# A decoder layer on one core: the second residual and its statistics, done for three batches of rows during the masked attention

## What is computed

```python
x = _layernorm(x + _L0_attn_ref(x, Wq, bq, Wk, bk, Wv, bv, Wf, bf))      # x1
x = _layernorm(x + _L0_xattn_ref(x, ctx, ctx, mask))                     # x2, the change is here
x = _layernorm(x + _L0_ffn_ref(x, w_gate, w_up, w_down))

def _layernorm(x, eps=1e-05):
    m, v = jnp.mean(x, -1, keepdims=True), jnp.var(x, -1, keepdims=True)
    return (x - m) / jnp.sqrt(v + eps)

def _L0_xattn_ref(q, k, v, mask):      # q = x1, k = v = context; per head of 32 columns
    scores = jnp.where(mask == 0, -1e9, einsum('bhqd,bhkd->bhqk', qh, kh) / sqrt(32))
    return einsum('bhqk,bhkd->bhqd', softmax(scores), vh)
```

## Time and profile before

| what | value |
|---|---|
| runs before | 3116.58, 3118.3, 3133.7 us; median 3118.3 |
| the profiled execution's own time | 3118.51 us |
| its span | 3116.7 us |
| mean granted TensorE clock | 0.935 |
| TensorE busy | 2617.6 us (84%) |
| VectorE busy | 2262.3 us (73%) |
| ScalarE busy | 1865.0 us (60%) |
| GpSimd busy | 1817.6 us (58%) |

### The profile page before, as it was taken

The page is one execution under the profiler, slowest core; times in us unless marked ns, Lnnn a source line. Parts: engine busy times, 40 slices in busy tenths (PEclk is TensorE's granted clock), DMA queues, the critical chain, the costliest instruction groups (busy, mean ns, idle before and its releaser), DMA issues. The chain is left out here.

```text
span 3116.7 us, 77411 instructions
## 1 busy us (share of the span) xinstructions
PE 2617.6 (84%) x24119; PEld 1411.1 (45%) x24119; DVE 2262.3 (73%) x4461; ACT 1865.0 (60%) x3767; POOL 1817.6 (58%) x1232
## 2 busy tenths in 40 slices
PE   7999578888886868999999999980999899703999
PEld 3555235555554434555555555540444344301444
DVE  8888667777775767788888888857433467697776
ACT  3444257777775435777777777764233577696333
POOL 3444479999997316999999999986100244300000
PEclk9999779999998988999999999995999999856999
DMA  8999824444445652122122232125544588797332
GB/s 303 337 335 339 271 97 135 132 128 134 128 137 163 242 199 69 53 82 69 52 85 61 56 97 55 44 59 183 206 162 161 194 271 288 252 415 279 112 124 81
DMA packets 324185, 513.52 MB, mean 165 GB/s; under 512 B 36757, under 2 KB 158485, under 8 KB 324074
## 3 DMA queue, kind: packets, MB, share of 16 engines
q1 hardware_dynamic: 320938, 505.88, 48.6%
q0 software_dynamic: 1952, 6.29, 0.6%
q10 hardware_dynamic: 1184, 0.01, 0.0%
HBM read 273.18 MB, written 194.28 MB: 150 GB/s over the span
## 5 line engine op out<-in xcount | busy, mean ns | idle before, releaser
L1164 POOL TENSOR_TENSOR cross_plo<-cross_p 128x2048 f16<-128x2048 f32 (+1 forms) x256 | 850.5, 3352 | 120.2 <-ACT cross_p L979 120.2
L1076 DVE CUSTOM_DVE_ANT_0 cross_junk<-cross_sc,rows 128x1024 bf16<-128x1024 f32 x512 | 622.7, 1223 | 159.2 <-PE cross_sc L865 149.7
L979 ACT ACTIVATE cross_p<-cross_st 128x512 f32<-128x512 f32 x1024 | 556.2, 595 | 205.4 <-PE cross_st L910 205.4
L1164 POOL TENSOR_TENSOR self_plo<-self_p 128x1024 f16<-128x1024 f32 (+7 forms) x512 | 577.3, 1166 | 18.7 <-ACT self_p L979 18.6
L979 ACT ACTIVATE self_p<-self_st,self_strip 128x512 f32<-128x512 f32 (+3 forms) x768 | 415.2, 582 | 148.0 <-PE self_st L908 117.2
L1076 DVE CUSTOM_DVE_ANT_0 self_junk<-self_sc,self_strip 128x1024 bf16<-128x1024 f32 (+7 forms) x512 | 371.1, 752 | 140.3 <-PE self_sc L871 135.3
L905 PE MATMUL cross_st<-cross_qa,cross_ka 97*128 97x512 f16 x1024 | 395.4, 386 | 2.4 <-ACT cross_p L979 1.9
L910 PE MATMUL cross_st<-rows,idbig 128*128 128x512 f16 x1024 | 391.0, 382 | 0.0
L934 PEld LDWEIGHTS cross_o<-cross_vh,cross_p 128*128 128x128 bf16 x4096 | 270.0, 97 | 76.3 <-issue 21.9
L934 PE MATMUL cross_o<-cross_vh,cross_p 128*128 128x65 f16 x4096 | 297.4, 191 | 5.1 <-POOL cross_plo L1164 4.7
L1774 POOL TENSOR_SCALAR v_w<-v_w 128x512 f32<-128x512 f32 x96 | 60.1, 626 | 401.5 <-ACT v_w L1751 401.4
(11 more groups left out here) (256 smaller groups left out, 5843.8 us busy)
## 6 DMA issues: line engine op xcount, KB each, us to landing
self_strip<-self_strips SPq DMA_DIRECT2D x68, 516.0 KB, 3.2
scr_gate<-gt_y SPq DMA_DIRECT2D x96, 256.0 KB, 2.1
v_w<-scr_gate SPq DMA_DIRECT2D x96, 256.0 KB, 4.1
scr_h<-v_w SPq DMA_DIRECT2D x96, 256.0 KB, 4.2
j_h<-scr_h SPq DMA_DIRECT2D x48, 512.0 KB, 9.5
d_o<-scr_o SPq DMA_DIRECT2D x9, 1536.0 KB
scr_up<-v_y SPq DMA_DIRECT2D x48, 256.0 KB, 4.3
j_u<-scr_up SPq DMA_DIRECT2D x24, 512.0 KB, 12.1
```

Source lines behind the costliest of these rows:

```text
L979: nc.scalar.activation(p32[j][:, b + q0 - a:b + q1 - a], stp[cc % 2][:, 0:q1 - q0], ACT.Exp, bias=bias, scale=SM).then_inc(expd, 1)
L1076: nc.vector.tensor_tensor_reduce(junk[slot % 2][:, 0:w], sc[slot % 2][:, 0:w], bias, 1.0, -3e38, ALU.add, ALU.max, qmax[n % 2][:, qt:qt + ...
L1164: nc.gpsimd.tensor_tensor(plo[j][:, a:z], p32[j][:, a:z], high, ALU.subtract).then_inc(lo_g, 1)
```

## The change

In rounds 5 to 16 of the masked attention (i = 4 to 15) two row tiles a round of the batch finished before get their residual and statistics: SyncE loads x1 of the tile at t = 8 and t = 20 (`load_row`), GpSimd adds it at t = 14 and t = 26 (`add_row`), VectorE takes bn_stats, bn_aggr and copies the two numbers into the new SBUF tensor `moments` at t = 22 and t = 31 (`statistics`). That is 24 tiles, the first three batches. `steps` splits the loop over rounds for the two engines that have row work. Its core:

```diff
+        ADD_AT, STAT_AT = {14: 0, 26: 1}, {22: 0, 31: 1}
+        def row_of(i, j):
+            return (i - H // HB) * 2 + j
...
+                def load_row(i, j):
+                    sp.wait_ge(row_added, row_of(i, j) + 1)
+                    sp.dma_start(x1b[j][:], x1_dram[ds(row_of(i, j) * P, P), :]).then_inc(x1_in[j], 16)
-                def step(i, t, last, next_batch=None, first=False):
+                def step(i, t, last, next_batch=None, first=False, with_row=False):
                     n, k = divmod(t, UH)
+                    if with_row and t in (8, 20):
+                        load_row(i, t // 20)
...
-                steps(dve, prologue, step)
+                def statistics(i, t):
+                    if t not in STAT_AT:
+                        return
+                    j = STAT_AT[t]
+                    r = row_of(i, j)
+                    dve.wait_ge(row_added, r + 3)
+                    nc.vector.bn_stats(bn[j][:], kept[:, ds(r, 1), :].rearrange("p o n -> p (o n)")).then_inc(row_stats, 1)
+                    dve.wait_ge(row_stats, r * 3 + 1)
+                    dve.sem_inc(stood, 1)
+                    nc.vector.bn_aggr(pair_of[j][:], bn[j][:]).then_inc(row_stats, 1)
+                    dve.wait_ge(row_stats, r * 3 + 2)
+                    nc.vector.tensor_copy(moments[:, ds(r * 2, 2)], pair_of[j][:]).then_inc(row_stats, 1)
+                steps(dve, prologue, step, None if causal else statistics)
...
-                steps(pool, prologue, step)
+                def add_row(i, t):
+                    if t not in ADD_AT:
+                        return
+                    j = ADD_AT[t]
+                    row = kept[:, ds(row_of(i, j), 1), :].rearrange("p o n -> p (o n)")
+                    pool.wait_ge(o_out, i * 16)
+                    pool.wait_ge(x1_in[j], (i - (H // HB - 1)) * 16)
+                    nc.gpsimd.tensor_tensor(row, row, x1b[j][:], ALU.add).then_inc(row_added, 1)
+                if not causal:
+                    pool.sem_inc(row_added, 2)
+                steps(pool, prologue, step, None if causal else add_row)
```

`second_norm_phase` then loads and adds only the last eight tiles (`NL`); the roots are taken in two operations, one over the 24 early tiles and one over the eight late ones, and ScalarE scales all 32 tiles in order:

```diff
+    NT, EARLY, TQ = T // P, (B - 1) * ST, 2
+    NL, NQ = NT - EARLY, NT // TQ
+    SECOND = 16
...
+                for n in range(NL):
+                    pool.wait_ge(t_in[n // TQ], 16)
+                    nc.gpsimd.tensor_tensor(rows(EARLY + n), rows(EARLY + n), b[:, n], ALU.add).then_inc(added, 1)
...
+                square_root(0)
+                for n in range(NT):
+                    if n == SECOND:
+                        square_root(1)
+                    if n in (0, EARLY):
+                        act.wait_ge(centred, n // EARLY + 1)
+                    nc.scalar.activation(rows(n), rows(n), ACT.Identity, scale=rs[:, n:n + 1], bias=nm[:, n:n + 1]).then_inc(scaled, 1)
...
+                centre(0)
+                for n in range(NL):
+                    statistics(n)
+                    if n % 2:
+                        largest(n // 2)
+                for g in range(NL // 2, NQ):
+                    if g == SECOND // TQ + 1:
+                        centre(1)
+                    largest(g)
```

More of the change, by code:

```diff
@@ L658, in attention_phase, with steps, batch_of @@
         KR = 3 * HD + (2 if causal else 1)
-        def steps(eng, prologue, step):
-            prologue()
[L665 to L671, removed]
+        def steps(eng, prologue, step, with_row=None):
+            def batch_of(i, last, with_row):
+                for t in range(HB * UH):
+                    step(i, t, last)
+                    if with_row is not None:
+                        with_row(i, t)
+            prologue()
+            batch_of(0, False, None)
+            if with_row is None:
+                with eng.Fori(1, NI - 1) as i:
+                    batch_of(i, False, None)
+            else:
+                with eng.Fori(1, H // HB) as i:
+                    batch_of(i, False, None)
+                with eng.Fori(H // HB, NI - 1) as i:
+                    batch_of(i, False, with_row)
+            batch_of(NI - 1, True, with_row)
+        ADD_AT, STAT_AT = {14: 0, 26: 1}, {22: 0, 31: 1}
+        def row_of(i, j):
+            return (i - H // HB) * 2 + j
         def to_finish(i, t, late):
@@ L1431, in _ @@
             def _(sp):
[L1432 to L1435, removed]
+                for j in range(NL // TQ):
+                    g = EARLY // TQ + j
+                    sp.dma_start(b[:, j * TQ:(j + 1) * TQ], x1_dram[g * (TQ * P):(g + 1) * (TQ * P), :].rearrange("(t p) n -> p t n", p=P)).then_inc(t_in[j], 16)
                 for dst, src in loads:
@@ L1441, in _, with square_root @@
             def _(pool):
[L1442 to L1445, removed]
+                for n in range(NL):
+                    pool.wait_ge(t_in[n // TQ], 16)
+                    nc.gpsimd.tensor_tensor(rows(EARLY + n), rows(EARLY + n), b[:, n], ALU.add).then_inc(added, 1)
             @block.scalar
             def _(act):
+                def square_root(j):
+                    if j == 1:
+                        act.wait_ge(stats, 2 * NL)
+                    nc.scalar.activation(sd[:, half(j)], mv[:, half(j), 1], ACT.Sqrt, bias=eps[:, 0:1]).then_inc(root, 1)
                 act.wait_ge(eps_set, 1)
[L1450 to L1457, removed]
+                square_root(0)
[5 more added lines that the diff above has]
+                    nc.scalar.activation(rows(n), rows(n), ACT.Identity, scale=rs[:, n:n + 1], bias=nm[:, n:n + 1]).then_inc(scaled, 1)
             @block.vector
```

81 lines of the change are left out of this document (39 added, 42 removed).

## The result

The kernel after the change takes 3151.4 us, median of 6 runs (3146.6 to 3162.1), against 3120.2 (3116.5 to 3133.7, 6 runs) before, measured beside it: a ratio of 1.0107, with a 95% interval of 1.0087 to 1.0127. It is slower by about 1%. The forecast was 3132.5 with a range up to 3150; it leaned to the slower side, rightly, but too little, and the median lies 1.4 us outside the range.

What follows compares the result with a forecast made beforehand. TensorE was taken to bound the attention, while nothing hides the normalisation stage. 3118.5 us, less 33.5 for that stage, plus 47.5 for waiting copies and the adds, gave 3132.5 us, range 3115 to 3150.

Steps and rivals of the forecast that it cites:

- Part 1: Second normalisation stage: the first 24 rows need only root and scale, so it gets 33.5 us shorter.
- Part 2: The 24 adds on GpSimd in the attention: hidden by its idle time except in the last round, 1.2 us.
- Part 3: The 24 statistics on VectorE: their two-column copy waits for GpSimd's running operation and delays the gather; 47.5 us with Part 2.
- rival (a): The two-column copy doesn't wait for GpSimd, so statistics cost little: 3095 us, faster; chance 0.15.
- Step 22: First statistics of a round: the waiting copy delays a maximum and the gather; TensorE loses 2.3 us, twelve times.
- Step 31: Second statistics of a round: the waiting copy delays the gather directly; TensorE loses 1.9 us, eleven times.
- The step that failed: TensorE's granted clock in the attention: assumed unchanged behind its short pauses, so nothing was added to the sum.
- The signs named: Trace marks foretold: norm stage 31 us, copies 1.3 to 2.5 us ending with GpSimd operations, rounds 60.5 us, adds 1.2 to 1.3.
- (b): The adds' time on GpSimd isn't regained and copies meet later boundaries, losing 3.1 and 2.5 us: 3148.5 us; chance 0.10.

Runs made afterwards that it cites:

- e2: The changed kernel with the 24 adds kept in the attention but their statistics put back in the norm stage; 3106.4 us, ratio 0.9956 to the kernel before.
- e1: The changed kernel with each two-column copy into the moments made as two one-column copies; 3102.2 us, ratio 0.9947 to the kernel before.
- e3: The changed kernel with the two-column copy at step 22 alone, one-column copies at step 31; 3146.6 us, ratio 1.0087 to the kernel before.
- e7: The changed kernel with one-column copies, first add at step 17 instead of 14, its statistics at 25 instead of 22; 3108.7 us, ratio 0.9963.
- e4: The changed kernel with the two-column copy at step 31 alone, one-column copies at step 22; 3120.3 us, ratio 1.0004 to the kernel before.
- e8: The changed kernel with one-column copies and the second statistics at step 29 instead of 31; 3090.8 us, ratio 0.9904 to the kernel before.
- e11: The changed kernel, two-column copy kept, with the destination's columns eight bytes apart instead of four; 3148.3 us in one run.
- e10: The changed kernel with statistics at steps 20 and 29, both columns moved by one two-input instruction instead of the copy; 3104.7 us, ratio 0.9962.

## Why the forecast was wrong

**Part 1, the norm stage, -33.5: right.** It runs from 2163.57 to 2195.26, 31.7 us instead of 64.7: -33.0. In the timeline of the kernel after the steps come as worked out, the root straight behind the table load, and VectorE last:

```profile
2164.86 0.32 ACT L1508 ACTIVATE s_sd<-moments,s_eps 128x24 f32<-128x24 f32 x1
...
2165.76 9.98 ACT L1517 ACTIVATE rows<-rows,s_nm,s_rs 128x512 f32<-128x512 f32 x14 [0.59 <-DVE s_nm L1528]
...
2187.09 7.97 DVE L1544 TENSOR_REDUCE s_tmax<-rows 128x1 f32<-128x1024 f32 x7
2195.09 0.17 DVE L1557 TENSOR_REDUCE pmax_x<-s_tmax 128x1 f32<-128x16 f32 x1
```

**Part 2, the adds, 1.2 us: right.** 1.27 us each, hidden in eleven rounds (e2), 1.7 us in the last round against 1.2. That they fill GpSimd to 620 of 621 us went beyond the forecast, in which a quarter of its idle time (3.3 less 2.45 us a round) was left.

**Part 3, the copy waits for GpSimd: right**, against rival (a), which e1 turned into a kernel: copies of 0.15 us, and 3102 us where it was priced at 3095, since its pause is 1.25 us and not 0.8 (0.45 us of idle VectorE between copies and gather stood in no term).

**Step 22, 2.3 us: right** (2.16, ends 1.9 and 3.1). Eleven rounds lost it, the number that the sum has once the last round is taken off.

**Step 31, 1.9 us: too high.** It is 1.73, then twice 1.54, then 1.12 us in the steady rounds, 12.7 us in all instead of 11 x 1.9 = 20.9. The sum had the copy meet a boundary of GpSimd after 1.2 us; in the steady rounds it is there after 0.44. And most of the pause is not the copy's wait: e1, e3 and e7 show 1.25 to 1.36 us with copies that don't wait at all, the price of the statistics right ahead of the gather; the wait of 1.32 us in e4 made it 1.74. Together the pauses cost 36.5 us, against 48.5 less 2.3 for the last round in the sum: the sum was 10 us too high here.

**The step that failed** is this one: "TensorE's clock stays out of the sum ... a shorter gap of the same kind doesn't change what comes behind it". It left out 23.2 us, the busy time that TensorE added with no matmul added, more than the 18.9 by which the median was missed (and the 14.1 by which the profiled execution was). Its evidence was a stretch in which TensorE was busy 36.86 of 40 us at full clock. That stretch has two pauses, of 1.60 and 1.54 us; it says nothing of one of 2.16 us, which the kernel before has in no round but the last. In the preparation it has three of that kind, 2.12 to 2.48 us long, and the clock stays full. But in the kernel after the same code, with pauses of 2.46 and 2.47 us, has a half-clock stretch of 3.4 us at the end of each. One of the three, in the kernel before and then in the kernel after, the matmul that ends it and the two microseconds from 127.00:

```profile
126.06 0.41 PE L364 MATMUL g_t<-idf,g_wq 128*128 128x128 f32 x2 [2.47 <-DVE w_q L507]
127.00:129.00 2.00, 2.00 (x12) 0.94 (x10) 1.97 (x5) 0.80 (x2) 0.87 (x1) 1.00 1.05 387
...
125.64 0.45 PE L364 MATMUL g_t<-idf,g_wq 128*128 128x128 f32 x1 [2.47 <-DVE w_q L507]
127.00:129.00 2.00, 2.00 (x7) 0.92 (x6) 1.93 (x5) 0.95 (x2) 1.29 (x2) 0.52 1.06 412
```

Over the thirteen traces 29 of 39 such pauses (1.92 to 2.48 us) have one, and e1, like the kernel before, has none. So the trace of the kernel before could not rule the fall out: behind a pause that left the clock alone in one execution, the clock can fall in the next. The term should have had two ends, nothing and half clock for some microseconds behind each pause. The experiments give the length: 3.4 us, 1.7 us lost. With TensorE's added idle time (37.2 us) and added busy time (23.2) as measured: 3118.5 - 33.0 + 37.2 + 23.2 + 1.7 - 1.0 = 3146.6, the profiled execution of after. Against the forecast that is 23.2 for the clock and some 9 less for the pauses.

The other runs of the kernel after lie 4 to 16 us higher. e4 suggests a part of it: where a pause of the same size sometimes costs a stretch of half clock and sometimes doesn't, runs differ by it. The mean clocks on record point that way, 0.931 for the profiled run and 0.929 for the two slowest, but 0.002 of 3150 us is some 6 us of the 16; the rest stays open.

**The signs named** were in part poor ones. "a round of 62 us proves (b)" would have misled: the steady round is 61.4, 5.0 above before, and would have passed for (b), adds whose time isn't regained, with pauses of 3.1 and 2.5. The pauses (2.16 and 1.12) rule that out, and so does e2. The copies, 2.7 and 0.44 us, lie outside the 1.3 to 2.5 us named on both sides, though they do end with GpSimd's operations.

**What stays open:** what decides at which pause of 1.74 us the clock falls. The traces of the rounds show only that the risk grows with the size: none up to 1.25, 6 of 10 at 1.74 in e4, 18 of 22 at 2.16, with the two of 1.54 that both had one out of line. An aggregation that writes straight into the table of moments, with no copy at all, was not tried.

## What to carry to other kernels

Before a small VectorE operation is put beside a busy GpSimd, ask whether it is one that waits for GpSimd: here two columns waited up to 2.7 us and one column never, so two one-column copies (0.3 us) replaced one that cost 49 us in all. Price a pause of a dense TensorE as the pause and the half-clock stretch that may follow it, and look for it in the granted clock of stretches of 2 us, since the share of busy time and the waits don't show it. A pause of that size that left the clock alone in one trace is no proof. And put side work where the engine has idle time ahead of its next consumer, not right ahead of the operation TensorE waits for: moving 1.2 us of statistics from step 31 to 29 was worth 11 us (e1 to e8).

## What was unexpected of the hardware

- The size at which an operation on VectorE begins to wait: one column from SBUF 0.15 us beside a busy GpSimd (144 to 156 ns, 48 of 48 in e1), two columns up to 2.7 us, also when they lie eight bytes apart (e11: 2.68).
- Two inputs in SBUF wait as one input of two columns does: 2.52 us for 256 numbers (e10). The Trainium skill, "SBUF — State Buffer", section "Who interferes with whom", states both, that an instruction with two SBUF inputs contends with a GpSimd instruction that reads SBUF, and that one with a single input outside the two-port modes doesn't. e10 agrees with the first. The copies of e1 agree with the second if one column is outside those modes; that they didn't wait is all that the runs show of it. The waits were whole here, up to the end of GpSimd's operation.
- TensorE around a single pause of 2.16 us in a stretch that is otherwise full: 1.2 GHz for 3.4 us (sometimes 6.8) in 18 of 22 cases (kernel after and e3), a loss of 1.7 us on top of the pause.
- A loss of the one kind can shrink another: as TensorE slowed, the copies of step 31 met GpSimd nearer to an end of its operations and fell from 1.31 us over 1.12 and 1.13 to 0.46 in the fourth round. In e4, without the pauses of step 22, they stayed at 1.31 to 1.32.
